# Fp8 layer norm: six of eight tiles moved into the attention's last steps, half the input scaled on ScalarE, the next norm in halves

## The reference

```
x = x + _L1_xattn_ref(_layernorm(x), ctx, ...)    # attention, 32 heads of 8
x = x + _L1_ffn_ref(_layernorm(x), w_fc, w_proj)  # the fp8 layer
x = x + _L2_xattn_ref(_layernorm(x), ctx, ...)    # small attention, keys and queries from ctx
x = x + _L2_ffn_ref(_layernorm(x), ...)           # attention with 16 heads, then experts
...
def _fp8_matmul(x2d, w):
    scale_x = jnp.maximum(jnp.max(jnp.abs(x2d)) / 448.0, 1e-06)
    scale_w = jnp.maximum(jnp.max(jnp.abs(w)) / 448.0, 1e-06)
    x8 = (x2d / scale_x).astype(float8_e4m3fn)
    w8 = (w / scale_w).astype(float8_e4m3fn)
    return (x8.astype(x2d.dtype) @ w8.astype(x2d.dtype).T) * (scale_x * scale_w)
h = jnp.square(jax.nn.relu(_fp8_matmul(x2d, w_fc)))
out = _fp8_matmul(h, w_proj)
```

## Time and profile before

| | |
|---|---|
| median of three runs | 1579.7 us (1578.46 to 1580.02) |
| the profiled execution | 1574.27 us |
| its span, first to last instruction | 1572.5 us |
| TensorE busy | 1337.8 us, 85% |
| VectorE busy | 1054.1 us, 67% |
| ScalarE busy | 755.9 us, 48% |
| GpSimd busy | 219.8 us, 14% |
| mean granted TensorE clock | 0.926 of full |

### The profile page before, as it was taken

How to read it: one execution, slowest core, us unless ns; L and a number is a source line. 1 busy time by engine, 2 the same in 40 slices (tenths; PEclk the granted TensorE clock), 3 DMA queues, 4 the chain that set the end, 5 groups by cost and what they waited for, 6 DMA issues and landing times.

```text
span 1572.5 us, 21463 instructions
## 1 busy us (share of the span) xinstructions
PE 1337.8 (85%) x6921; PEld 936.1 (60%) x6929; DVE 1054.1 (67%) x2197; ACT 755.9 (48%) x1882; POOL 219.8 (14%) x221
## 2 busy tenths in 40 slices
PE   6787759986998556899999779994999999869998
PEld 3444435553444224577776669983888888754554
DVE  6888877888666388678778543225666666566564
ACT  3677822445776463755555212223666666512221
POOL 3122320000000000212221064111111112010000
PEclk9899979995899977999999879997999999968999
DMA  4222140000000200000002179854112211110100
GB/s 152 94 94 94 67 190 5 0 1 2 4 4 5 78 0 1 0 1 34 33 2 61 54 261 337 299 212 140 68 67 67 73 67 60 34 51 17 33 33 27
DMA packets 36274, 111.02 MB, mean 71 GB/s; under 512 B 4677, under 2 KB 15950, under 8 KB 30848
## 3 DMA queue, kind: packets, MB, share of 16 engines
q1 hardware_dynamic: 34320, 105.75, 18.9%
q0 software_dynamic: 1872, 4.22, 0.7%
HBM read 84.66 MB, written 26.21 MB: 71 GB/s over the span
## 4 chain that ended last, share of the span: by engine, by line
PE 67%; DVE 17%; issue 6%; ACT 6%; DMA 2%; POOL 1%; SPq 1%; DVEq 0%; ACTq 0%; POOLq 0%
PE psum L2919 6%; PE psum L2250 4%; PE psum L1832 4%; PE psum L817 4%; PE psum L2578 4%; PE psum L2526 4%; PE psum L2556 3%; PE psum L1874 3%; PE psum L2604 3%; DVE roomA L697 3%; PE psum L2929 3%; PE psum L2259 2%; PE psum L1274 2%; PE psum L1864 2%; PE psum L851 2%
## 5 line engine op out<-in xcount | busy, mean ns | idle before, releaser
L2643 ACT ACTIVATE roomA<-psum,roomA 128x256 f32<-128x256 f32 x128 | 70.9, 559 | 92.6 <-DVE roomA L2708 92.3
L1441 DVE TENSOR_REDUCE roomB<-psum 128x2 f32<-128x512 f32 x128 | 83.8, 688 | 37.4 <-PE psum L1274 36.5
L1920 ACT ACTIVATE roomA<-psum,roomA 128x128 f32<-128x128 f32 (+1 forms) x128 | 53.3, 427 | 88.4 <-DVE roomA L1995 88.2
L2919 PE MATMUL psum<-roomA,roomB 128*128 128x512 f32 (+1 forms) x192 | 91.9, 623 | 0.3 <-ACT roomA L3026 0.3
L2379 DVE SCALAR_TENSOR_TENSOR roomA<-roomA,psum 128x512 f32<-128x512 f32 x23 | 15.9, 689 | 102.0 <-ACT roomA L2294 102.0
L1832 PE MATMUL psum<-own,roomB 128*128 128x512 f32 x160 | 76.7, 605 | 3.5 <-DVE roomA L1987 2.1
L494 PE MATMUL psum<-roomB,own 128*128 128x256 f32 x256 | 65.7, 408 | 15.8 <-ACT roomB L577 15.8
L1795 POOL TENSOR_TENSOR roomA<-roomA 128x512 f32<-128x512 f32 x40 | 50.8, 1270 | 177.4 <-DVE roomA L1988 170.4
L494 PEld LDWEIGHTS psum<-roomB,own 128*128 128x128 f32 x256 | 51.8, 205 | 37.8 <-ACT roomB L577 21.5
L2578 PE MATMUL psum<-roomA 128*128 128x256 f32 x256 | 68.3, 389 | 6.0 <-DVE roomA L2720 4.4
L697 DVE TENSOR_TENSOR_SCAN roomA<-roomA 128x1024 f32<-128x1024 f32 x32 | 73.1, 2284 | 0.0
(11 more groups left out here) (497 smaller groups left out, 3386.3 us busy)
## 6 DMA issues: line engine op xcount, KB each, us to landing
roomB<-m_w_dram SPq DMA_DIRECT2D x12, 1536.0 KB, 9.0
roomA<-m_w_dram SPq DMA_DIRECT2D x11, 1536.0 KB, 8.7
a_kv_ready<-roomB SPq DMA_DIRECT2D x32, 512.0 KB, 3.1
roomA<-a_kv_ready SPq DMA_DIRECT2D x8, 1024.0 KB, 4.8
roomA<-a_kv_ready SPq DMA_DIRECT2D x16, 512.0 KB, 4.1
roomB<-a_w_dram SPq DMA_DIRECT2D x4, 1280.0 KB, 6.2
roomB<-f_w_dram SPq DMA_DIRECT2D x8, 624.0 KB, 3.8
m_rows<-roomA SPq DMA_DIRECT2D x1, 2978.5 KB, 16.0
```

Source lines behind the costliest of these rows:

```text
L1441: dve.tensor_reduce(maxneg[:, hp // 8, :, m, hp % 8], g.bank(m).rearrange("p (q k) -> p q k", k=S), AX.X, ALU.max, negate=True).then_inc(s ...
L2919: ins = pe.matmul(g.bank(bank, rows=m), w[:, kt, at:at + m], xg[:, n % 2, kt, half * HALF:(half + 1) * HALF], start=(kt == 0), stop=(kt == ...
```

## The change

It has four parts.

1. In attn1's VectorE loop, from step 70 (`EARLY`), tiles 0 to 5 are measured (step 70), the root taken and three tiles normalised (72), three more (74), and the largest value of the six taken (76). The normalised tiles go to `xn`, memory of `hT`, whose earlier tenant is read no more once `a1_tr` stands at 32.
2. Behind the last add, VectorE does the same for tiles 6 and 7 only; ScalarE normalises none.
3. The first half is rounded as before. For the second, ScalarE makes two scaled copies (L1631 and L1632 of the kernel after, in the order of its queue behind the four query and key copies), and VectorE needs three instructions.
4. attn2 uses `norm_halves`, with the first half's products (`sums`) between the two halves of transposes. ffn1's four adds move into that norm, and the wait of ScalarE, VectorE and TensorE between the two layers goes.

```diff
+    EARLY = max(OUT_STEP[0:3]) + 3
...
+            if n == EARLY:
+                dve.wait_ge(s["layer_done"], base + 3)
+                g.f1_norm["measure"](dve, 0, 6)
+            if n == EARLY + 2:
+                g.f1_norm["root"](dve, 0, 6)
+                dve.wait_ge(s["a1_tr"], 8 * B)
+                g.f1_norm["apply"](dve, 0, 3)
+            if n == EARLY + 4:
+                g.f1_norm["apply"](dve, 3, 6)
+            if n == EARLY + 6:
+                g.f1_norm["largest"](dve, 0, 6, 0)
...
+    xn = hT.rearrange("p f t -> p (f t)")[:, 0:NT * D].rearrange("p (i d) -> p i d", d=D)
+    sides = room.take(2)
...
     def scalar(act):
+        act.wait_ge(s["f1_amax"], 2)
+        act.activation(tmp2[:, 1], flat(xn[:, 4:8]), ACT.Copy, scale=sides[:, 1:2])
+        act.activation(tmp1[:, 1], flat(xn[:, 4:8]), ACT.Copy, scale=sides[:, 0:1]).then_inc(s["f1_scaled"], 1)
...
     def vector(dve):
         step = g.dve_steps
-        dve.tensor_reduce(amax[:, 0:1], flat(g.XN), AX.X, ALU.max, apply_absolute_value=True).then_inc(s["f1_amax"], 1)
+        measure(dve, 6, NT)
+        root(dve, 6, NT)
+        apply(dve, 6, NT)
+        largest(dve, 6, NT, 3)
+        dve.tensor_tensor(amax[:, 0:1], amax[:, 0:1], amax[:, 3:4], ALU.max).then_inc(s["f1_amax"], 1)
         dve.wait_ge(s["f1_allmax"], 2)
         step(dve.tensor_scalar(scale[:, 0:1], allmax[:, 0:1], 1 / FP8_MAX, 1e-6, ALU.mult, ALU.max))
         step(dve.reciprocal(inv[:, 0:1], scale[:, 0:1]))
+        step(dve.tensor_scalar(sides[:, 0:1], inv[:, 0:1], -1.0, None, ALU.mult))
+        dve.tensor_scalar(sides[:, 1:2], inv[:, 0:1], 2.0 ** 20, None, ALU.mult).then_inc(s["f1_amax"], 1)
+        quantise(dve, step, flat(x8[:, 0:4]), flat(xn[:, 0:4]), inv[:, 0:1], tmp1[:, 0], tmp2[:, 0]).then_inc(s["f1_x8"], 1)
+        t1, t2 = tmp1[:, 1], tmp2[:, 1]
+        dve.wait_ge(s["f1_scaled"], 1)
+        step(dve.tensor_scalar(t2.bitcast(U32), t2.bitcast(U32), 0x7F800000, 0x00400000, ALU.bitwise_and, ALU.bitwise_or))
+        step(dve.scalar_tensor_tensor(t1, t2, 1.5 * LOW * 2 ** 20, t1, ALU.max, ALU.add))
+        dve.wait_ge(s["f1_x8"], 1)
+        dve.scalar_tensor_tensor(flat(x8[:, 4:8]), t2, 1.5 * LOW * 2 ** 20, t1, ALU.max, ALU.subtract).then_inc(s["f1_x8"], 1)
         step(dve.memset(zeros, 0.0))
-        for half in range(2):
-            t = slice(4 * half, 4 * half + 4)
-            quantise(dve, step, flat(x8[:, t]), flat(g.XN[:, t]), inv[:, 0:1], tmp1[:, half], tmp2[:, half])\
-                .then_inc(s["f1_x8"], 1)
...
-    return [dict(sync=sync, tensor=tensor_qk, scalar=scalar_qk)] + norm(g, transposed=False) + [
+    g.last_adds = [lambda dve, k=k: add(dve, k) for k in range(4)]
+    return [dict(sync=sync, tensor=tensor_qk, scalar=scalar_qk)] + [
         dict(gpsimd=gpsimd, tensor=tensor, scalar=scalar, vector=vector)]
...
-    head = norm(g)
+    head = norm_halves(g, between=lambda pe: sums(pe, 0))
...
-    return head + [dict(tensor=tensor)]
+    return head + [dict(tensor=lambda pe: sums(pe, 1))]
```

More of the change, by code:

```diff
@@ L1522, in ffn1, with measure, root, apply @@
     flat = lambda a: a.rearrange("p a b -> p (a b)")
+    xn = hT.rearrange("p f t -> p (f t)")[:, 0:NT * D].rearrange("p (i d) -> p i d", d=D)
+    sides = room.take(2)
+    def measure(dve, a, z):
+        for i in range(a, z):
+            ins = dve.bn_stats(out=g.stats[:, i, :], in_=g.X[:, i, :])
+        g.dve_steps(ins)
+        for i in range(a, z):
+            ins = dve.bn_aggr(out=g.mv[:, i, :], in_=g.stats[:, i, :])
+        g.dve_steps(ins)
+    def root(dve, a, z):
+        g.dve_steps(rsqrt_two(dve, g.dve_steps, g.rstd[:, a:z], g.var[:, a:z], g.t8a[:, a:z], g.t8b[:, a:z], 1e-5, g.mv[:, a:z, 1]))
+    def apply(dve, a, z):
+        for i in range(a, z):
+            ins = dve.tensor_scalar(xn[:, i, :], g.X[:, i, :], g.mv[:, i, 0:1], g.rstd[:, i:i + 1], ALU.subtract, ALU.mult)
+        g.dve_steps(ins)
+    def largest(dve, a, z, at):
+        g.dve_steps(dve.tensor_reduce(amax[:, at:at + 1], flat(xn[:, a:z]), AX.X, ALU.max, apply_absolute_value=True))
+    g.f1_norm = dict(measure=measure, root=root, apply=apply, largest=largest)
     def sync(sp):
@@ L1656, in vector @@
             t1, t2 = tmp1[:, f % 4], tmp2[:, f % 4]
-            dve.wait_ge(s["f1_scaled"], f + 1)
+            dve.wait_ge(s["f1_scaled"], f + 2)
             step(dve.tensor_scalar(t2.bitcast(U32), t2.bitcast(U32), 0x7F800000, None, ALU.bitwise_and))
@@ L1662, in vector, with add @@
         dve.reciprocal(t_inv, total).then_inc(s["a2_inv"], 1)
[L1663 to L1669, removed]
-    return [dict(sync=sync, tensor=tensor_qk, scalar=scalar_qk)] + norm(g, transposed=False) + [
+    def add(dve, k):
+        dve.wait_ge(s["f1_out"], k + 1)
+        xs = g.X[:, 2 * k:2 * k + 2, :].rearrange("p i d -> p (i d)")
+        dve.scalar_tensor_tensor(xs, g.bank(k), prod[:, 1:2], xs, ALU.mult, ALU.add).then_inc(s["layer_done"], 1)
+        return s["layer_done"], base + k + 1
+    base = g.done_count
+    g.done_count += 4
+    g.last_adds = [lambda dve, k=k: add(dve, k) for k in range(4)]
+    g.last_done = lambda dve, sem, count: None
+    return [dict(sync=sync, tensor=tensor_qk, scalar=scalar_qk)] + [
         dict(gpsimd=gpsimd, tensor=tensor, scalar=scalar, vector=vector)]
@@ L1676, in attn2, with sums @@
     s, attT = g.sem, g.a2_attT
-    def tensor(pe):
-        pe.wait_ge(s["a2_attT"], B)
-        for i in range(NT):
+    def sums(pe, half):
+        pe.wait_ge(s["a2_attT"], 2 * half + 2)
+        pe.wait_ge(s[("xt_first", "xt_ready")[half]], xt_done)
+        for i in range(4 * half, 4 * half + 4):
             b = i // 2
-            if i % 4 == 0:
-                pe.wait_ge(s[("xt_first", "xt_ready")[i // 4]], xt_done)
             for kt in range(2):
```

## The result

The changed kernel takes 1574.36 us (median of 20 runs, 1562.40 to 1578.61), the kernel before, on the same chip, 1582.18 us (20 runs, 1569.0 to 1587.98). The ratio is 0.995 with a 95% interval of 0.993 to 0.9969. Timed a second time, on the chip of the last three experiments, it was 1573.55 against 1580.11, ratio 0.9955 [0.9929, 0.9982]. So it is faster by 6.6 to 7.8 us; 7.6 was forecast. The forecast median was 1572.1 us, the stated range 1567.5 to 1577.5; 1574.36 lies in it. The kernel before was also 2.5 us slower in its 20 runs than in the first three, from which the forecast started.

A forecast was written before the change was run, and what follows sets the result against it. TensorE was taken to carry 67% of the chain (VectorE 17%), with VectorE the chain in the front. 9.2 us gained there less 1.6 lost in the halved norm made 7.6: median 1572.1 us from 1579.7, range 1567.5 to 1577.5.

The forecast's parts named there:

- The front: From the attention's last add to the end of the second rounding: VectorE's shorter chain gains 9.2 us, bounds 8.4 to 10.9.
- the bound taken (0.68): First of VectorE's three second-half rounding instructions: 0.68 us as with one bit operation, or 1.22 as for the maximum.
- the upper end of 10.9: Largest front gain, 10.9 us, if the first projection ran at the high clock level from the first.
- The work moved into the attention: Attention's last steps: 8.3 us of VectorE work cost nothing, hidden by its waits for TensorE; bounds 0 or all 8.3.
- The cover of the first block: Statistics and aggregates of six tiles end 1.0 us ahead of the `keep` at 517.39, the smallest cover left.
- The norm in halves: From ffn1's first add to the next norm's first-half aggregates: 19.5 us against 17.9 before, a cost of 1.6.
- the bounds of 18.3 and 22.6: Halved norm with transposes and products all at the high clock (cost 0.45 us) or all at the low (4.7).
- the lucky 17.87: Length in us before the change, ffn1's first add to the next norm's statistics, against which the halved norm was priced.
- The predicted 1.6: Cost in us of the halved norm of attn2, with 6 of 16 product records at the low clock level.
- wrong if the last add moves by over 1 us: Sign against the forecast: the attention's last add, near 533.4 us, should stay unmoved.
- The two yardsticks: Old lengths taken from the trace: VectorE's front chain, 23.06 us from 534.11, and the plain norm, 17.87 us.
- the clock behind 632 us: Rival: shifted TensorE bursts lower the later clock; a mean 0.01 lower returns 6.6 us, 0.02 gives 1585.4; chance 0.05.

The follow-up runs named there:

- e4: Parts 1 to 3 without part 4, with nothing moved into the attention (all eight tiles handled behind the last add): 1574.29 us, ratio 0.9974 to the kernel before.
- e5: Parts 1 to 3 without part 4 and without ScalarE's scaled copies; VectorE rounds the second half by itself: 1572.00 us, ratio 0.9952 to the kernel before.
- e7: Parts 1 to 3 without part 4, plus two unread scaled copies on ScalarE ahead of the two that count: 1572.51 us, ratio 0.9954 to the kernel before.
- e2: The kernel before with part 4 of the change alone: 1580.49 us, ratio 0.9997 to the kernel before.
- e6: Parts 1 to 3 without part 4, with the six early tiles' statistics and aggregates taken three times over: 1572.74 us, ratio 0.9954 to the kernel before.
- e9: The changed kernel, unaltered, run again: 1573.55 us, ratio 0.9955 to the kernel before.
- e1: The changed kernel without part 4, attn2's norm left whole: 1573.33 us, ratio 0.9945 to the kernel before.
- e10: Parts 1 to 3 of the change alone, attn2's norm left whole, run a second time: 1571.98 us, ratio 0.993 to the kernel before.
- e8: The changed kernel with the last copy to XT of attn2's norm on ScalarE in place of VectorE: 1569.01 us, ratio 0.9935 to the kernel before.
- e11: The changed kernel with attn2's last copy to XT on ScalarE, run a second time: 1569.12 us, ratio 0.9923 to the kernel before.
- e3: The changed kernel with all of TensorE's transposes in attn2's norm first, then all products: 1571.95 us, ratio 0.9947 to the kernel before.

## Why the prediction was right

**The front.** Every step came where it was laid, counted from the start of the statistics:

| | predicted | measured |
|---|---|---|
| scale at VectorE | 5.13 | 5.07 |
| first rounding starts | 5.81 | 5.72 |
| end of ScalarE's second copy | 10.52 | 10.53 |
| second rounding ends | 13.85 | 13.76 |
| gain | 9.2 | 9.30 |

The form that the trace of before lacked, two bit operations in one, took 0.69 us: the bound taken (0.68), not the other (1.22). The first projection did not become faster, as the upper end of 10.9 supposed: 45.25 us from the front's end to ffn1's first add, 45.21 before. e4, e5 and e7 take the front apart, and each came within 0.3 us of its expectation. How much the old front would have taken was less certain than I made it: e2 has 25.42 for it.

**The work moved into the attention.** It is hidden. The cover of the first block was 1.02 us (1.0 predicted). But the step was too strict in one point: it took the smallest of the three gaps as what hides the work. e6 shows that a block may overrun its gap, since `keep`s that are late but still ahead of the last TensorE result delay nothing. What counted here is the sum of the gaps up to the last `keep`: e6 used all but 0.50 us of it. No run goes beyond it.

**The norm in halves.** The mechanism was right: the second transposes stand behind the products, and VectorE's add behind its copy. The size was off in one term, the clock of the first sixteen products: 4.75 us predicted with six of them low, measured 6.63 (6.68 in e9). With 3.69 us at the high level and about twice that at the low, some four fifths of the burst ran low. The transposes ahead of it ran high and gave back 0.7 us. So the aggregates came at 20.46 instead of 19.5, within the bounds of 18.3 and 22.6. Against the lucky 17.87 this is a cost of 2.6 us, against the same norm undivided behind the same front (e1, e10) 1.0 and 1.1, in e2 2.05. The predicted 1.6 lies among them, but its two sides were both too low: the new norm because of the clock in the products, the old one because 17.87 was the lowest of seven.

The granted clock in these products was 0.53. The windows of e9, over the first transposes, the products and what follows:

```profile
603.60:604.70 1.10, 1.07 (x8) 0.86 (x8) 1.06 (x6) 0.38 (x1) 0.00 (x0) 1.00 0.00 0
605.54:612.06 6.52, 6.52 (x16) 5.18 (x17) 1.65 (x9) 1.09 (x2) 0.00 (x0) 0.53 0.00 0
612.06:617.60 5.54, 4.67 (x25) 3.75 (x23) 4.26 (x15) 0.59 (x1) 0.00 (x0) 1.00 0.00 0
```

TensorE had idled 2.88 us, ran eight transposes at 1.00, paused 0.82 us, and then ran at half rate. The Trainium skill, "TensorE: Matmul & The Clock Gate", section "Loop structure matters more than you think", has a long DMA wait between matmuls as its bad case, after which the array is slow. This row fits it loosely: the pause is 0.82 us, for a copy on ScalarE. The pause is not shown to be the cause here: e1, whose burst is unbroken, was granted 0.50 over the same stretch behind ffn1's first add. The low level lay there with the split and without it; that the split brought it about, no run shows. What the slow products cost depends on what hangs on them. In e8 they are just as slow and the norm is 2.8 us shorter, since VectorE's adds no longer wait for the copy behind them. VectorE still waits there for the products themselves, 2.04 and 1.37 us before its first two adds.

**What the prediction got by luck.** The sum fits the medians, 7.6 against 7.8 and 6.6, but the sign "wrong if the last add moves by over 1 us" did come up: the tail was 23.82 against 20.27. The mechanism behind that sign, VectorE delaying the `keep`s, is refuted by their waits and by e6. The tail is TensorE at 0.50. Whether the early work makes that level likelier stays open. Seven of ten profiled executions with early work have a long tail, none of the three without it; but nine of the ten (all but e6) run the same instructions up to the last add and show 20.27, 20.28, 22.54 to 22.56 and 23.82, and e8 and e11 are one and the same kernel. The clock had also gone other ways before any early work: in the 30 us ahead of the third add PEclk was 0.77 in all six executions with a tail of about 22.5, and 1.00 in before, e4, e6, e11 and the kernel after, though e2 and e3 had 0.77 too and a short tail. If the early work does bring the low level, it gives back 2.3 to 3.5 us each time.

The two yardsticks also come from one execution. The old front, 23.78 in it, was 25.42 in e2, and the plain norm, 17.87 in it, was up to 19.50. With the longer ones the front would gain more and the halved norm cost less. And the prediction took the profiled execution to lie 5.4 us under the median before and after; after, it lay 0.6 us above. So the mechanisms are borne out stretch by stretch, but that 7.6 falls between 6.6 and 7.8 is in part luck.

The rival "the clock behind 632 us" was not seen in this pair. From the first rotation behind the norm (631.10 and 631.40) to the end it is 941.40 and 941.80, at PEclk 0.95 in both.

## The scatter between runs follows the granted clock

I had taken the spread of three runs, 1.6 us, for the noise of a measurement. In 94 runs the kernel before spreads from 1569.2 to 1595.4 us. Within one kernel the time follows the mean granted TensorE clock of the run: the correlation is -0.95 in the 94 runs of before and -0.94 in 32 runs of the change. A common slope fitted within each kernel, over the 235 runs of before, the change and the experiments, is 10.6 us less for each 0.01 of clock (95%: 10.0 to 11.1), and leaves 1.8 us of scatter. The two profiled executions are 0.007 apart, which by this slope is 7.4 us: nearly all that the change gains. The stretches agree: the first 513 us and the tail, which are 3.33 and 3.55 us longer at a lower clock with the same TensorE work, make 6.9. That is why the two came out alike (1574.27 and 1574.92). The fit cannot replace the medians, since the change also removes time in which the clock was low, and so moves the mean clock itself: 0.918 before, 0.921 after.

## What to carry to other kernels

Cut two traces at the same instructions and compare the pieces: most stretches repeat to 0.1 us, or differ by a visible step of the clock, where a whole run scatters by 20, and a piece with no changed instruction tells how much of a difference is the clock. When work is moved into an engine's waits, look for the first result that is really needed: in e6 the sum of the waits up to it hid the work, though two single waits were overrun. When a norm or any step is split into halves, look at what stands in front of the consumer in its own queue: here one 0.69 us copy held the adds back by 4 us, and giving it to ScalarE, which was idle, brought more (2.8 us) than the split cost (1.0 us at the same place of the clock). Without that step the halved norm (19.92 to 20.52 us) was above every plain one (17.87 to 19.50).
